# Feed-forward widening as three fp32r products in a Perceiver kernel; x kept in the output's place during the layers

## The reference

```python
def ffn_layer(x, g, bln, W1, b1, W2, b2):
    mu = x.mean(-1, keepdims=True)
    var = ((x - mu) ** 2).mean(-1, keepdims=True)
    xn = (x - mu) / jnp.sqrt(var + 1e-05) * g + bln
    hg = xn @ W1 + b1                      # W1: (256, 2 * 682)
    a, gate = jnp.split(hg, 2, -1)
    return a * jax.nn.gelu(gate, approximate=False) @ W2 + b2
...
x = x + _L0_ffn_ref(_layernorm(x, axis=-1), ...)   # six layers inside; their sum is added to x
```

## Time and profile before

| | us |
|---|---|
| median of the runs | 2193.85 |
| the profiled execution | 2194.99 |
| its span | 2193.2 |
| TensorE busy | 2094.9 |
| Vector busy | 1681.2 |
| Scalar busy | 1340.5 |
| GpSimd busy | 512.1 |

### The profile page before, as it was taken

One profiled execution on the slowest core, in us unless ns is written; L12 is line 12 of the kernel. 1 busy time (PEld: TensorE's weight loads), 2 busy tenths in 40 slices (PEclk: granted clock), 3 DMA queues, 4 the chain that ended last, 5 costly groups with the idle time before them and its releaser, 6 DMA issues.

```text
span 2193.2 us, 49531 instructions
## 1 busy us (share of the span) xinstructions
PE 2094.9 (96%) x16360; PEld 1704.0 (78%) x16360; DVE 1681.2 (77%) x4797; ACT 1340.5 (61%) x3916; POOL 512.1 (23%) x291
## 2 busy tenths in 40 slices
PE   3899999999999898999999999999999999999988
PEld 3687787787786676888888878888888888888877
DVE  5777667677575587898889888887889888988882
ACT  1666656656655245676667666766667666766652
POOL 2020110111011242232223222232223222322220
PEclk9999999999999999999999999999999999999999
DMA  3000000000000400020112011201120111111000
GB/s 117 7 8 3 6 7 5 6 7 6 6 26 0 154 11 13 13 70 13 32 51 70 14 33 52 71 14 33 52 71 13 30 47 51 33 32 52 14 13 20
DMA packets 46853, 70.00 MB, mean 32 GB/s; under 512 B 9077, under 2 KB 33573, under 8 KB 46373
## 3 DMA queue, kind: packets, MB, share of 16 engines
q1 hardware_dynamic: 44261, 62.21, 9.4%
q10 hardware_dynamic: 2368, 4.98, 0.6%
HBM read 50.54 MB, written 1.05 MB: 24 GB/s over the span
## 4 chain that ended last, share of the span: by engine, by line
PE 53%; DVE 4%; issue 3%; DMA 2%; ACT 2%; POOL 2%; SPq 0%; DVEq 0%; ACTq 0%; POOLq 0%
PE ps_loc L1549 17%; PE ps_loc L1655 9%; PE ps_loc L1626 6%; PE ps_loc L1665 4%; PE ps_loc L1599 4%; PE ps_loc L1588 4%; PE ps_loc L1615 4%; PE ps_loc L1568 3%; DMA late<-y_all 2%; POOL rnorm L2456 1%; PE ps_loc L1209 1%; DVE norm L2078 1%; ACT prob_loc L1878 0%; DVE w_low L2070 0%; PE ps_loc L1637 0%
## 5 line engine op out<-in xcount | busy, mean ns | idle before, releaser
L2456 POOL TENSOR_TENSOR rnorm<-norm_floor,half_loc 128x32 f32<-128x32 f32 x48 | 300.3, 6257 | 584.3 <-DVE norm_floor L2081 461.2
L1549 PE MATMUL ps_loc<-w_high,xT 128*128 128x512 f32 x1152 | 379.3, 410 | 0.7 <-ACT qk L1857 0.6
L1878 ACT ACTIVATE prob_loc<-prob_loc,top_loc 128x128 f32<-128x128 f32 x768 | 298.5, 398 | 46.1 <-DVE top_loc L2145 43.9
L1655 PE MATMUL ps_loc<-xnT_loc,w 128*128 128x256 f32 (+1 forms) x1056 | 251.1, 383 | 2.4 <-DVE kT_loc L2213 1.2
L673 ACT ACTIVATE prob<-prob,new_top 128x256 f32<-128x256 f32 x512 | 252.1, 497 | 0.0
L1549 PEld LDWEIGHTS ps_loc<-w_high,xT 128*128 128x128 f32 x1152 | 203.5, 188 | 50.6 <-issue 9.3
L2145 DVE CUSTOM_DVE_ANT_0 prob_loc<-ps_loc,const,rnorm 128x128 f32<-128x128 f32 x768 | 218.7, 345 | 27.2 <-PE ps_loc L1588 25.5
L855 DVE CUSTOM_DVE_ANT_0 prob<-ps_cross,bias 128x256 f32<-128x256 f32 x512 | 184.9, 420 | 67.5 <-PE ps_cross L455 52.9
L1870 ACT ACTIVATE qT_loc<-ps_loc 128x512 f32<-128x512 f32 x96 | 57.3, 597 | 292.9 <-PE ps_loc L1568 292.9
L1549 PE MATMUL ps_loc<-w_low,xT 128*128 128x512 f32 x576 | 227.4, 395 | 0.0
L1655 PEld LDWEIGHTS ps_loc<-xnT_loc,w 128*128 128x128 f32 (+1 forms) x1056 | 190.2, 189 | 28.3 <-DVE kT_loc L2213 2.6
(11 more groups left out here) (200 smaller groups left out, 4315.2 us busy)
## 6 DMA issues: line engine op xcount, KB each, us to landing
w_raw<-in_ffn_Wqkv_dram SPq DMA_DIRECT2D x24, 512.0 KB, 5.7
w_raw<-in_ffn_Wqkv_dram SPq DMA_DIRECT2D x24, 256.0 KB, 4.0
wo<-in_ffn_Wo_dram SPq DMA_DIRECT2D x24, 256.0 KB, 3.7
v_mid<-v_even SPq DMA_DIRECT2D x24, 256.0 KB, 3.3
v_mid<-v_odd SPq DMA_DIRECT2D x24, 256.0 KB, 3.7
w<-in_ffn_W_dram SPq DMA_DIRECT2D x12, 341.0 KB, 4.7
w<-in_ffn_W_dram SPq DMA_DIRECT2D x6, 640.0 KB, 5.6
ctx_raw<-in_ctx_dram SPq DMA_DIRECT2D x12, 256.0 KB, 2.8
```

The source lines that it names most:

```text
L1549: ins = pe.matmul(ps[:, DENSE + j % 2, :], xT[:, px, kk, t * P:(t + 1) * P], wqkv[pw][:, kk, col:col + 512], start=kk == 0 and n == 0, sto ...
L1655: ins = pe.matmul(ps[0:n, DENSE + m % 2, part * T:(part + 1) * T], w1[:, kk, col:col + n], xnT[:, kk, :], start=kk == 0, stop=kk == KD - 1)
L1878: ins = act.activation(pr, pr, ACT.Exp, bias=top[:, h, t:t + 1], scale=-1.0, accum_out=total[:, h, t:t + 1])
L2456: pool.tensor_tensor(rnorm[:, b % 2, t, :], norm2_floor[:, :], half[:, :], ALU.pow).then_inc(rnorm_done, 8)
```

## The change

1. w1 gets the treatment that wqkv has: it is loaded raw (in the place of its low part), copied to a high part (fp32r) by Scalar and the difference to a low part by Vector, in four pieces of 682 columns, at the end of slot b = 0 of each layer.
2. The transposed xn is written twice by Scalar for each half, as fp32r high part and in full; Vector writes the difference as low part (`xn_low`).
3. `widen` multiplies high by high, low by high and high by low, three fp32r matmuls in place of one fp32 matmul.
4. Vector's `sums(n, 0)` is cut in two halves of 1024 columns, the first behind `share(a, 5)`, the second behind `share(a, 6)`.
5. For room, x is written to the output's DRAM before the layers and read back at the last layer into the place of w_high; xn, its parts and `gate` stand where x stood. b2 is loaded for one layer at a time, behind w1.

```diff
@@ place_layer_weights
+        with ExitStack() as shared:
+            self.x_back = self.sb("x_back", [P, B * TT, D], F32, shared)
         self.w_high = self.sb("w_high", [P, KD, 3 * INNER], F32R)
...
-        self.w1 = self.sb("w1", [P, KD, GATE_MAIN + FF - REST])
+        with ExitStack() as shared:
+            self.w1_raw = self.sb("w1_raw", [P, KD, W1_WIDE], F32, shared)
+        self.w1_low = self.sb("w1_low", [P, KD, W1_WIDE], F32R)
...
@@ SyncE
             def ffn_weights(L, i):
                 sp.wait_ge(f_full, L)
                 k.load_layer_weights(sp, i, "w1")
+                sp.wait_ge(b2_done, L)
+                k.load_layer_bias(sp, i)
                 sp.wait_ge(f2_full, L)
                 k.load_layer_weights(sp, i, "w2")
...
             middle(LAYER, 0)
+            sp.wait_ge(y_out, 2 * LAYER)
+            sp.dma_start(out, k.x[:, :, :]).then_inc(out_done, 16)
             layer(LAYER, 0, True, False)
...
+            sp.wait_ge(qkv_done, (LAYERS + 1) * LAYER)
+            sp.wait_ge(out_done, 16)
+            sp.dma_start(k.x_back[:, :, :], out).then_inc(out_done, 16)
...
@@ TensorE, widen
                 if m == 0:
                     if b == 0:
-                        pe.wait_ge(w1_in, a + LAYER)
-                    pe.wait_ge(xnT_done, a + U)
+                        pe.wait_ge(w1_low_done, a + LAYER)
+                    pe.wait_ge(xn_wide, a + U)
+                    pe.wait_ge(xnT_done, a + U // 2)
...
                     for kk in range(KD):
-                        ins = pe.matmul(ps[0:n, DENSE + m % 2, part * T:(part + 1) * T], w1[:, kk, col:col + n], xnT[:, kk, :],
-                                        start=kk == 0, stop=kk == KD - 1)
+                        if m == 0 and part == 0 and kk == 1:
+                            pe.wait_ge(xnT_done, a + U)
+                        for i, (pw, px) in enumerate(PARTS):
+                            ins = pe.matmul(ps[0:n, DENSE + m % 2, part * T:(part + 1) * T], w1[pw][:, kk, col:col + n],
+                                            xnT[px][:, kk, :], start=kk == 0 and i == 0, stop=kk == KD - 1 and i == 2)
@@ Scalar
                 for kk in range(KD):
-                    ins = act.activation(xnT[:, kk, :], ps[:, DENSE, kk * T:(kk + 1) * T], ACT.Identity,
-                                         bias=vec[:, V_FB + kk:V_FB + kk + 1], scale=vec[:, V_FG + kk:V_FG + kk + 1])
-                ins.then_inc(xnT_done, U)
+                    for dst in (xnT[HIGH], xnT_wide):
+                        ins = act.activation(dst[:, kk, :], ps[:, DENSE, kk * T:(kk + 1) * T], ACT.Identity,
+                                             bias=vec[:, V_FB + kk:V_FB + kk + 1], scale=vec[:, V_FG + kk:V_FG + kk + 1])
+                    ins.then_inc(xn_wide, U // 2)
+
+            def widening_high(L, p, first):
+                if p == 0:
+                    act.wait_ge(w1_in, L + LAYER)
...
+                kk, cols = w1_piece(p)
+                act.activation(w1[HIGH][:, kk, cols], w1_raw[:, kk, cols], ACT.Copy).then_inc(w1_high_done, LAYER // 4)
...
                 if ffn:
                     gates(f, 4)
                     gates(f, 5)
+                if b == 0:
+                    for p in range(4):
+                        widening_high(L, p, not ffn)
@@ Vector
+            def xn_low(a):
+                for kk in range(KD):
+                    dve.wait_ge(xn_wide, a + U // 2 * (kk + 1))
+                    dve.tensor_tensor(xnT[LOW][:, kk, :], xnT_wide[:, kk, :], xnT[HIGH][:, kk, :], ALU.subtract)\
+                        .then_inc(xnT_done, U // 2)
+
+            def widening_low(L, p, first):
+                dve.wait_ge(w1_high_done, L + LAYER // 4 * (p + 1))
...
+                dve.tensor_tensor(w1[LOW][:, kk, cols], w1_raw[:, kk, cols], w1[HIGH][:, kk, cols], ALU.subtract)\
+                    .then_inc(w1_low_done, LAYER // 4)
...
                 inverse(a, 6)
+                share(a, 5)
                 if ahead:
-                    sums(n, 0)
-                share(a, 5)
+                    sums_early(n, 0)
+                if ffn:
+                    xn_low(f)
...
                 share(a, 6)
+                if ahead:
+                    sums_late(n, 0)
...
                 add_attention(a, b)
+                if b == 0:
+                    for p in range(4):
+                        widening_low(L, p, not ffn)
                 if not ahead:
                     moments(a, b, None, last=True)
                 if ffn:
                     add_ffn(f, fb)
```

More of the change, by code:

```diff
@@ L44 @@
 GATE_MAIN = GATE_REST + REST
+W1_WIDE = GATE_MAIN + FF - REST
+W1_CUTS = (slice(0, FF), slice(GATE_REST, W1_WIDE))
+W1_PAD = slice(FF, GATE_REST)
 WINDOW = 64
@@ L143, in __init__ @@
         self.ctx = ctx
-        self.x = self.sb("x_all", [P, B * TT, D])
+        self.x_place = ExitStack()
+        self.x = self.sb("x_all", [P, B * TT, D], ctx=self.x_place, side="right")
         self.y = self.sb("y_all", [P, B * TT, D])
@@ L201, in load_layer_weights @@
             for kk in range(KD):
-                eng.dma_start(self.w1[:, kk, 0:FF], src[one, :, kk, 0:FF].rearrange("o p n -> (o p) n")).then_inc(self.w1_in, 16)
+                eng.dma_start(self.w1_raw[:, kk, 0:FF], src[one, :, kk, 0:FF].rearrange("o p n -> (o p) n")).then_inc(self.w1_in, 16)
             for at, cut in ((GATE_MAIN, slice(FF, 2 * FF - REST)), (GATE_REST, slice(2 * FF - REST, 2 * FF))):
-                eng.dma_start(self.w1[:, :, at:at + cut.stop - cut.start], src[one, :, :, cut].rearrange("o p k n -> (o p) k n"))\
+                eng.dma_start(self.w1_raw[:, :, at:at + cut.stop - cut.start], src[one, :, :, cut].rearrange("o p k n -> (o p) k n"))\
                     .then_inc(self.w1_in, 16)
@@ L210, in load_layer_weights, with load_layer_bias @@
                     .then_inc(self.w2_in, 16)
+    def load_layer_bias(self, eng, i):
+        src = self.io["ffn_b2"].rearrange("(o i) d -> i o d", o=1)[bass.ds(i, 1)]
+        for j in range(4):
+            cut = slice(j * D // 4, (j + 1) * D // 4)
+            eng.dma_start(self.b2[:, 0, cut], src[:, 0, cut].broadcast_to([P, D // 4])).then_inc(self.b2_in, 16)
     def load_layer_vectors(self, eng):
@@ L1164, in linear_parts @@
      yn_ready, ynT_full, ynT_done, x_full, x_done) = k.lin_counts
-    ln_var, ln_rstd, dve_step, half_set, dve_held = (
-        sem(f"lin_{n}") for n in ("ln_var", "ln_rstd", "dve_step", "half_set", "dve_held"))
+    ln_var, ln_rstd, dve_step, half_set = (sem(f"lin_{n}") for n in ("ln_var", "ln_rstd", "dve_step", "half_set"))
+    dve_held = k.dve_held
     def sync(sp):
@@ L1416, in local_layers @@
         pT = sb("pT", [P, 2, 2, TT, P])
-        xn = sb("xn_loc", [P, TT, D])
-        xnT = sb("xnT_loc", [P, KD, T])
-        gate = sb("gate", [P, 2, T])
+        w1 = (sb("w1_high", [P, KD, W1_WIDE], F32R), k.w1_low)
         k.lin_place.close()
+        k.x_place.close()
+        xn = k.sb("xn_loc", [P, TT, D], F32, ctx, "right")
+        with ExitStack() as shared:
+            xnT_wide = k.sb("xnT_wide", [P, KD, T], F32, shared, "right")
+        xnT_low = k.sb("xnT_low", [P, KD, T], F32R, ctx, "right")
+        xnT = (k.sb("xnT_high", [P, KD, T], F32R, ctx, "right"), xnT_low)
+        gate = k.sb("gate", [P, 2, T], F32, ctx, "right")
         qT = k.sb("qT_loc", [P, PAIRS, T], F32, ctx, "right")
@@ L1432, in piece, with w1_piece @@
             return kk, slice(c * 512, (c + 1) * 512)
+        def w1_piece(p):
+            kk, part = divmod(p, 2)
+            return kk, W1_CUTS[part]
         def ring(pair):
@@ L2106, in cosines, with sums_early, sums_late @@
                     .then_inc(cos_done if s else q_cos_done, 8 if s else U)
+            def sums_early(a, t):
+                dve.wait_ge(cos_done, a + 8 * t + 8)
+                dve.tensor_tensor(qk[:, t, 0:INNER], qk[:, t, 0:INNER], work[:, 1, 0:INNER], ALU.add)
+            def sums_late(a, t):
+                dve.wait_ge(cos_done, a + 8 * t + 8)
+                dve.tensor_tensor(qk[:, t, INNER:], qk[:, t, INNER:], work[:, 1, INNER:], ALU.add).then_inc(sum_done, 8)
             def sums(a, t):
@@ L2206, in normal @@
                 ins.then_inc(xn_done, U)
+            def xn_low(a):
[5 more added lines that the diff above has]
+                dve.wait_ge(w1_high_done, L + LAYER // 4 * (p + 1))
+                if p == 0 and first:
+                    dve.tensor_tensor(w1[LOW][:, :, W1_PAD], w1_raw[:, :, W1_PAD], w1[HIGH][:, :, W1_PAD], ALU.subtract)
+                kk, cols = w1_piece(p)
+                dve.tensor_tensor(w1[LOW][:, kk, cols], w1_raw[:, kk, cols], w1[HIGH][:, kk, cols], ALU.subtract)\
+                    .then_inc(w1_low_done, LAYER // 4)
             def gated(a, m):
@@ L2231, in _, with slot @@
              first_y) = linear_vector(dve)
-            def slot(L, b, i, shifts, ffn, ahead, turn, split=False, late=False, first=False):
```

(7 more changed lines are left out.)

62 lines of the change are left out of this document (34 added, 28 removed).

## The result

The changed kernel takes 2273.56 us (median of four runs, 2270.42 to 2276.44) beside 2194.29 us for the kernel before (median of four). The ratio is 1.0354, 95% interval 1.0337 to 1.0371: slower by 79 us, where 79 were forecast. The profiled execution took 2270.42 us, with a span of 2268.6 us, 75.4 longer than before.

A forecast was written before the change was run, and what follows sets the result against it. TensorE was taken to set the time, with Vector 6 to 10 us from being late. Stall +72.5, clock +12.5, layer 0 +2, slot savings -8 gave +79: 2274 us profiled, 2272.5 as median, range 2248 to 2296.

The forecast's parts named there:

- The stall: Boundary after slot b = 0, layers 1 to 5: late w1 holds Scalar, Vector and TensorE 14.5 us each, 72.5 us.
- One link: SyncE's queue at the boundary: the shift's two issues last 0.76 and 4.79 us ahead of the loads of w1.
- The clock: Behind each of the five stalls TensorE runs at a lowered clock: 2.5 us a boundary, 12.5 in all.
- The saving inside the slots: Net 0.6 us in 13 slots and 0.1 in five with split weights, 8 us; b = 0 in layers 1 to 5 nothing.
- 1.51 was forecast: Widening on TensorE: a group of twelve fp32r matmuls at 126 ns each, about 1.5 us.
- 31 were forecast: TensorE's widening with three fp32r matmuls a product: 1.3 us less a slot, 31 us for 24 widenings.
- The 58 us: Widening by passes alone, about four to three: a quarter of 9.61 us, 2.4 us a slot, 58 us in all.
- the rival in which TensorE keeps its saving: Stall as forecast, but 1.3 to 2.4 us a slot stay won in 18 to 19 slots: 2237 to 2257 us; 8%.
- Layer 0: No stall, since w1 is there long before; `widening_low` (3.4 us) ahead of `k_out` costs about +2 us.
- Covered edits: b2 by layer costs 0, or 1 us a layer if late; x to the output and back 0; tail's two sums 0.
- The sum: Whole kernel: +72.5 + 12.5 + 2 - 8 = +79 on 2194.99 us, 2274 us; as median of runs 2272.5 us.

The follow-up runs named there:

- Experiment 1: Changed kernel with SyncE issuing the four loads of w1 ahead of the shift of y, not behind it; 2190.74 us, ratio 0.9979.
- experiment 2: Kernel before, plus only a wait of Scalar for w1 at the end of the queue of slot b = 0; 2263.43 us, one run.
- experiment 4: Also written `row_first`: changed kernel with the shift's one-row transfer first, then the loads of w1, then the wide transfer; 2249.68 us, one run.
- experiment 3: Also written `row_behind`: changed kernel with the shift's one-row transfer put behind the loads of w1; 2274.71 us, one run.
- experiment 6: `piece_behind` with only the high by high product of the widening made, Scalar's and Vector's work kept; output not the reference's; 2178.95 us, ratio 0.9925.
- experiment 7: `piece_behind` with xn as its high part alone: one Scalar write, no Vector difference, no product with low xn; output not the reference's; 2164.37 us, ratio 0.9860.
- piece_behind: Experiment 1's kernel with the last of Vector's four low parts of w1 moved behind `k_out` of the next slot; 2187.60 us, ratio 0.9957.
- sums_whole: `piece_behind` with the sums again one instruction of 2048 columns ahead of `share(a, 5)`; 2191.09 us, ratio 0.9979.

## Why the prediction was right, and where its parts were off

**The stall** was the step that mattered, and it came as worked out: 14.6 us at a boundary against 14.5, five boundaries, and none in layer 0. Each link is in the rows above: the load's place in SyncE's queue, the landing, Scalar's copies (2.76 us for four, 3.0 forecast), Vector's differences (3.21 us), `add_ffn`, the fourth group of turns. Experiment 1 takes the lateness away and with it the whole loss; experiment 2 puts the wait alone into the kernel before and gets 67 us of the loss; experiment 4 shortens the lateness by 5 us and gets 5 us a boundary back.

**One link was misread.** The prediction lists 4.79 us as the issue of the shift's one-row transfer. Experiments 3 and 4 show that the time goes to any issue behind the wide transfer. The sum did not depend on it, but a mending built on it would have failed, as `row_behind` did.

**The clock** was taken as 2.5 us a boundary and came to 2.3: TensorE works for 23.4 us of the five stretches at half clock, and half of that is 11.7 (12.5 forecast). The boundary shown has 1.9. That the low clock lasts 13.7 us and costs only 1.9 is because most of it falls on the pause itself. The slots of b = 1 grew by 82.6 us; 72.9 of stall and 11.7 of clock are 84.6, so they gained 2.0 inside.

**The saving inside the slots** was put at 8 us. The layers outside layer 0's first two slots give 7.5: 2.0 in the slots of b = 1 of layers 1 to 5, 3.1 in those of b = 0, to which the prediction gave nothing, and 2.4 in those of b = 2 and 3, to which it gave 4.7. That is right in sum but not by kind, so in part luck. The reasons hold. In the slot ahead of the boundary shown (b = 0):

```profile
1313.40 0.36 PE L1692 MATMUL ps_loc<-xnT_high,w_high 128*128 128x256 f32 x1
...
1314.98 0.44 PE L1648 MATMUL ps_loc<-pT,v_even 128*64 128x128 f32 x4
...
1316.92 0.39 PE L1692 MATMUL ps_loc<-xnT_high,w_high 128*128 128x256 f32 x1 [0.23 <-DVE kT_loc L2284]
```

A piece of twelve takes 1.58 us from its start to the next line's; 1.51 was forecast, and TensorE waits 0.23 us for `gated(0)` ahead of the third. Vector there:

```profile
1311.39 0.43 DVE L2268 TENSOR_TENSOR xnT_low<-xnT_wide,xnT_high 128x256 fp32r<-128x256 f32 x1 [0.35 <-ACT xnT_wide L1939]
...
1315.25 1.22 DVE L2163 TENSOR_TENSOR qk<-qk,work 128x1024 f32<-128x1024 f32 x1
1316.38 0.48 DVE L2284 SCALAR_TENSOR_TENSOR kT_loc<-ps_loc,vec,gate 128x256 f32<-128x256 f32 x1
```

`xn_low`'s second half waits for Scalar's fourth pass, the late sums stand ahead of `gated(0)`. TensorE itself was spared some 24 us where 31 were forecast: its busy time is 14.0 us less, although 21 us more of it lie at half clock, which would be 10.5 less at full. About a third of the 24 arrives. Experiments 6 and 7 show that this is Scalar's and Vector's doing: at full clock 5.3 us a slot less on TensorE are worth 0.5, while their own 1.7 us a slot (with 2.7 of TensorE's) are worth 0.8. The Trainium skill (FP8 and Floating Point Precision, TensorE Precision Notes) gives four passes through the array for true fp32. The 58 us that the prediction worked out from three in place of four are shown by no slot here, and the rival in which TensorE keeps its saving (2237 to 2257 us) is out.

**Layer 0** was put at +2 us. Vector's `k_out` comes later there:

```profile
864.98 3.20 DVE L2276 TENSOR_TENSOR w_low<-w_raw,w_high 128x682 fp32r<-128x682 f32 x4
868.10 1.28 DVE L2187 COPY kT_loc<-ps_loc 128x512 f32<-128x512 f32 x2
```

The four differences run up to 868.1, and the turns end 6.0 us after their start in place of 5.1, +0.9: they are slow there anyway, at half clock, and cover half of it. The first two slots together are even 0.9 us shorter than before, so this term of the sum was wrong by 3 us.

**Covered edits.** GpSimd waits 64.3 us in 24 times ahead of its sum with b2, where the kernel before waits 64.5: at the boundary shown the last part of b2 is issued at 1343.5 and the sum begins at 1365.25. No engine's wait is put down to x on its way to the output and back. `piece_behind` has both edits and is faster than the kernel before, so together they cost less than what it gains; that they cost nothing was not measured apart.

**The sum.** In the profiled executions the terms are +72.9 for the stall, +11.7 for the clock, -7.5 inside the slots, -0.9 for layer 0 and -0.8 ahead of the layers, where two kernels that differ only in the layers can be as far apart (812.51 us in `piece_behind`, 811.28 in `sums_whole`): +75.4, where +79 was forecast. The medians are 79.3 apart because the profiled execution is the fastest of the four of the changed kernel. The stall, nine tenths of the whole, was right to 0.4 us; that the medians meet the forecast to the microsecond is luck. (2193.85 + 79 is 2272.85, not 2272.5 as the prediction has it.)

## What to carry to other kernels

When work is hung on a load, look up where the load stands in its queue, not how long it takes: here nobody had needed w1 for 30 us, so it stood behind a transfer that waits for the end of the slot and landed 11 us into the next one; a wait for it at the slot's end then held up Scalar, Vector and TensorE, 15 us in each of five layers. A saving on the busiest engine is worth only as much as the others leave: price what they do in exchange by the slot, since 1 us on the second busiest can take back most of it. Compare such prices at the same granted clock, slot by slot. And work put into an engine's idle time ahead of a wait is cheap only there; moved from ahead of `gated(0)` to behind `gated(1)` the same work cost 20 us.

## What the runs showed of the hardware

- The issue that comes right behind the wide transfer of the shift (127 rows, 127 KB) on SyncE's queue takes 4.5 to 6.4 us whatever it is: the one-row transfer 4.7 to 4.9 us in place of 0.55, the first load of w1 4.5 to 4.9 in place of 0.36 (`row_behind`), the load of wo 4.5 to 4.9 in place of 0.4 to 0.6 and the first of b2's four 6.0 to 6.4 in place of 0.35 (`row_first`). An issue that comes 22 us or more behind it takes its usual 0.35 to 0.53 us (`row_first`). Why is not shown.
- A pause of TensorE of 14.6 us takes the granted clock to 0.50 for 13.7 to 17.1 us in all, counted from inside the pause; at the five boundaries 3.6 to 5.9 us of it fell on work, so that it cost 1.8 to 3.0 us each.
